# Expert stage of a transformer block: the second layer too by seven products of tiles in place of eight

## The reference, cut to what matters

```
h = jax.nn.relu(jnp.einsum('ecd,edf->ecf', buf, w1) + b1[:, None, :])          # d = 256, f = 1024
y = (jnp.einsum('ecf,efd->ecd', h, w2) + b2[:, None, :]) * (1.0 - MOE_TOKEN_DROPOUT)   # dropout 0.2
return g1[:, None] * y1 + g2[:, None] * y2
```

## Time and profile before

| | us |
| --- | --- |
| runs | 5859.25, 5866.38, 5866.96; median 5866.38 |
| the profiled execution | 5857.93, its span 5856.2 |
| busy, of the span | PE 5507.3 (94%), PEld 4313.5 (74%), DVE 4335.1 (74%), ACT 3283.8 (56%), POOL 2037.6 (35%) |
| second layer's matmuls (L1489) | 926.0, 15% of the chain that ended last |
| one gather on POOL (L1663), mean | 1.05 |
| mean granted TensorE clock | 0.985 |

### The profile page before, as it was taken

The page is one execution under the profiler, slowest core; times in us unless marked ns, Lnnn a source line. Parts: engine busy times, 40 slices in busy tenths (PEclk is TensorE's granted clock), DMA queues, the critical chain, the costliest instruction groups (busy, mean ns, idle before and its releaser), DMA issues. The chain is left out here.

```text
span 5856.2 us, 150644 instructions
## 1 busy us (share of the span) xinstructions
PE 5507.3 (94%) x45977; PEld 4313.5 (74%) x45977; DVE 4335.1 (74%) x11737; ACT 3283.8 (56%) x7315; POOL 2037.6 (35%) x1753
## 2 busy tenths in 40 slices
PE   0999999979999999799999999977899999999998
PEld 0677777757777777567777777753788888888887
DVE  7889898868888888588888888879555555455554
ACT  4788888746666666477777777747223232232322
POOL 0222222223333333234444444430334343333433
PEclk9999999989999999899999999998999999999999
DMA  5777777646666666466676767642322222222221
GB/s 154 180 181 182 183 184 182 169 135 175 173 173 175 174 173 175 115 166 181 168 181 169 179 170 180 170 113 2 71 54 41 52 50 39 51 48 41 55 38 24
DMA packets 625563, 750.63 MB, mean 128 GB/s; under 512 B 131075, under 2 KB 554188, under 8 KB 625328
## 3 DMA queue, kind: packets, MB, share of 16 engines
q1 hardware_dynamic: 568992, 679.62, 44.3%
q0 software_dynamic: 49152, 63.10, 6.7%
q10 hardware_dynamic: 7184, 5.00, 0.4%
HBM read 476.49 MB, written 272.24 MB: 128 GB/s over the span
## 5 line engine op out<-in xcount | busy, mean ns | idle before, releaser
L1489 PE MATMUL exp_res<-exp_w,exp_hT 128*128 128x256 f32 x4096 | 926.0, 380 | 0.0
L1489 PEld LDWEIGHTS exp_res<-exp_w,exp_hT 128*128 128x128 f32 x4096 | 769.8, 190 | 97.9
L1682 POOL DMA_INDIRECT out_dram<-exp_gated,exp_token x256 | 406.2, 1587 | 990.8 <-issue 357.0
L931 DVE TENSOR_REDUCE F_tops<-F_score 128x2 f32<-128x512 f32 x1024 | 684.4, 687 | 60.8 <-PE F_score L685 41.1
L822 ACT ACTIVATE F_probs<-F_scoreT 128x512 f32<-128x512 f32 x1024 | 583.7, 590 | 235.8 <-PE F_scoreT L654 235.8
L931 DVE TENSOR_REDUCE A_tops<-A_score 128x3 f32<-128x384 f32 x1024 | 531.6, 554 | 63.7 <-PE A_score L671 55.5
L1545 ACT ACTIVATE exp_lone<-exp_lead 128x256 f32<-128x256 f32 x256 | 98.3, 384 | 766.5 <-PE exp_lead L1499 747.9
L822 ACT ACTIVATE A_probs<-A_scoreT 128x384 f32<-128x384 f32 x1024 | 451.2, 488 | 23.5 <-PE A_scoreT L642 14.9
L1539 ACT ACTIVATE exp_hT<-exp_hT,exp_b 128x512 f32<-128x512 f32 x512 | 339.3, 712 | 92.6 <-DVE exp_hT L1625 92.6
L654 PE MATMUL F_scoreT<-QS,KS 98*128 98x256 bf16 x2048 | 365.3, 275 | 9.6 <-ACT F_probs L822 1.5
L685 PE MATMUL F_score<-KS,QS 96*128 96x256 bf16 x2048 | 363.4, 275 | 8.7 <-DMA KS<-d_k 7.8
(11 more groups left out here) (357 smaller groups left out, 14519.1 us busy)
## 6 DMA issues: line engine op xcount, KB each, us to landing
QS<-d_q SPq DMA_DIRECT2D x384, 192.0 KB, 3.6
KS<-d_k SPq DMA_DIRECT2D x256, 192.0 KB, 4.0
QS<-d_q SPq DMA_DIRECT2D x384, 128.0 KB, 3.9
KS<-d_k SPq DMA_DIRECT2D x256, 128.0 KB, 4.0
d_q<-A_q_parts SPq DMA_DIRECT2D x64, 384.0 KB, 3.5
d_k<-A_k_parts SPq DMA_DIRECT2D x64, 384.0 KB, 3.8
QS<-d_q SPq DMA_DIRECT2D x384, 64.0 KB, 3.6
d_q<-X_q_parts SPq DMA_DIRECT2D x64, 384.0 KB, 3.9
```

Source lines behind the costliest of these rows:

```text
L931: nc.vector.tensor_reduce(dst, src, AX.X, ALU.max).then_inc(score_read, 1)
L1489: last = mm(res[t][:, s, :], hT[par][:, f, (2 * t + s) * P:(2 * t + s + 1) * P], w2[k][:, f, :], start=begin and f == fs[0], stop=f == BY_ ...
L1682: nc.gpsimd.indirect_dma_start(out, bass.IndirectOffsetOnAxis(token[j % (2 * XB)][:, s:s + 1], 0), gated[par][:, s, :], None, bounds_check ...
```

## The change

The second layer gets the same scheme as the first. Rows are taken in halves of 256 (two row tiles q), the 1024 inner columns in halves of four tiles (u, u + 4), the 256 output columns in halves of 128. A product of halves is 4 x 2 matmuls with 128 moving columns (`add`), and there are seven of them. `fold_second` makes the four sums `w2s` of quarters of `w2` once an expert (in chunk 5 for the next one; `fold_weights` moves from chunk 6 to chunk 4). `raise_sums` makes four sums `hTs` of quarters of `hT` each chunk: for tiles 0 to 2 in operations of 768 columns, then for tile 3 in operations of 256. The PSUM tiles `lead[0]` and `corner` are used again for the second layer, beside new `side_r` and `last_r` in place of `res`. ACT copies `lead[0]` out twice (`lone_r`, `pair_r`), takes over the two copies of `turn` from DVE (`copy_half`) and the four multiplications by the gate (`weigh`), which it does in the next chunk. DVE joins the four quarters of `y` with six sums, and scales `y` in place (`scale_rows`), the second half of it in the next chunk. ACT's last turn of the loop is peeled. Constants used before the expert stage move to an inner allocation (`program`), which makes room for the new tiles.

```diff
-        res = [ps(f"res{i}", [P, 2, 256]) for i in range(2)]
+        side_r, last_r = ps("side_r", [P, 2, HR]), ps("last_r", [P, 2, HR])
...
# PE
+                        def rows_of(f, half):
+                            return lambda q: hT[par][:, f, half * HR + q * P:half * HR + (q + 1) * P]
+                        def sums_of(s, u):
+                            return lambda q: hTs[:, s, u, q * P:(q + 1) * P]
+                        def tile(f, d):
+                            return w2[k][:, f, d * P:(d + 1) * P]
+                        def add(region, weights, moving, begin=False, end=False):
+                            for q in range(2):
+                                last = mm(region[:, q * P:(q + 1) * P], weights(q), moving, start=begin and q == 0, stop=end,
+                                          skip_group_check=True)
                             return last
+                        def straight(u):
+                            pe.wait_ge(hid_read, NF * n + 2 * u + 1)
+                            add(lead[0], rows_of(u, 0), tile(u, 0), u == 0)
+                            pe.wait_ge(hid_read, NF * n + 2 * u + 2)
+                            return add(corner, rows_of(u + HF, 0), tile(u + HF, 0), u == 0, u == HF - 1)
+                        def outer(u, ready, begin=False):
+                            pe.wait_ge(raised, 8 * n + ready)
+                            add(side_r[:, 0, :], sums_of(0, u), w2s[k][:, 0, u, :], begin, u == HF - 1)
+                            pe.wait_ge(raised, 8 * n + ready + 1)
+                            add(side_r[:, 1, :], sums_of(2, u), w2s[k][:, 2, u, :], False, u == HF - 1)
...
-                        need(pe, res_read, 2 * n)
-                        products(0, 0, BY_PAIR[0:4], True)
+                        need(pe, pair_kept, HF * n + HF - 1)
+                        need(pe, corner_read, HF * n + HF)
+                        for u in range(HF - 1):
+                            straight(u)
                         close(HF - 1)
-                        products(0, 0, BY_PAIR[4:6], False)
                         if another(n):
                             rows_here(r, j + 1)
                             turn_half(j + 1, n + 1, 0)
-                        products(0, 1, BY_PAIR[0:6], False)
-                        products(0, 0, BY_PAIR[6:8], False)
-                        products(0, 1, BY_PAIR[6:8], False).then_inc(res_full, 1)
+                        if c == 0:
+                            pe.wait_ge(folded2, 4 * e + 4)
+                        need(pe, res_read, 2 * n)
+                        for u in range(HF - 1):
+                            outer(u, 1, u == 0)
+                        straight(HF - 1).then_inc(res_led, 1)
+                        outer(HF - 1, 5)
                         if another(n):
                             turn_half(j + 1, n + 1, 1)
-                        products(1, 0, BY_PAIR, True)
-                        products(1, 1, BY_PAIR, True).then_inc(res_full, 1)
+                        pe.wait_ge(res_kept, n + 1)
+                        pe.wait_ge(raised, 8 * n + 7)
+                        for u in range(HF):
+                            last = add(lead[0], sums_of(1, u), w2s[k][:, 1, u, :], False, u == HF - 1)
+                        last.then_inc(res_full, 1)
+                        pe.wait_ge(raised, 8 * n + 8)
+                        for u in range(HF):
+                            add(last_r[:, 0, :], sums_of(3, u), tile(u + HF, 1), u == 0, u == HF - 1)
+                        for u in range(HF):
+                            last = add(last_r[:, 1, :], rows_of(u + HF, 1), w2s[k][:, 3, u, :], False, u == HF - 1)
+                        last.then_inc(res_closed, 1)
# ACT
+                            if u == 1 and earlier:
+                                weigh(n - 1, 1 - par, 0)
                             if u > 1:
                                 rectify(u - 2)
+                            if u == 2 and earlier:
+                                weigh(n - 1, 1 - par, 1)
...
                         rectify(HF - 2)
+                        if another(n):
+                            copy_half(n + 1, 1 - par, 0)
                         rectify(HF - 1)
+                        act.wait_ge(res_led, n + 1)
+                        need(act, res_corner, n)
+                        nc.scalar.activation(lone_r[:, :], lead[0][:, :], ACT.Copy).then_inc(res_kept, 1)
+                        if another(n):
+                            copy_half(n + 1, 1 - par, 1)
+                        act.wait_ge(res_full, n + 1)
+                        need(act, res_read, 2 * n)
+                        nc.scalar.activation(pair_r[:, :], lead[0][:, :], ACT.Copy).then_inc(res_pair, 1)
# DVE
+                def raise_sums(n, par, us, done, which):
+                    a11, a12 = hT[par][:, us, 0:HR], hT[par][:, us.start + HF:us.stop + HF, 0:HR]
+                    a21, a22 = hT[par][:, us, HR:NS], hT[par][:, us.start + HF:us.stop + HF, HR:NS]
+                    m = [hTs[:, i, us, :] for i in range(4)]
+                    if which == 0:
+                        v.tensor_tensor(m[0], a21, a22, ALU.add).then_inc(raised, 1)
+                        v.tensor_tensor(m[2], a11, a21, ALU.subtract).then_inc(raised, 1)
+                    else:
+                        dve.wait_ge(raised, 8 * n + done + 1)
+                        v.tensor_tensor(m[1], m[0], a11, ALU.subtract).then_inc(raised, 1)
+                        dve.wait_ge(raised, 8 * n + done + 3)
+                        v.tensor_tensor(m[3], a12, m[1], ALU.subtract).then_inc(raised, 1)
...
+                            if u == 0 and not (isinstance(n, int) and n == 0):
+                                scale_rows(n - 1, k if c else 1 - k, 1 - par, 1)
+                            if u == 0 and isinstance(n, int) and n == 0:
+                                fold_second(0, 0)
                             if u < HF - 1:
                                 first_corner(n, par, u + 1)
+                            else:
+                                dve.wait_ge(hid_read, NF * n + NF - 2)
+                                raise_sums(n, par, slice(0, HF - 1), 0, 0)
                             dve.wait_ge(closed, HF * n + u + 1)
...
-                        if another(n):
-                            copy_half(n + 1, 1 - par, 0)
+                        raise_sums(n, par, slice(0, HF - 1), 0, 1)
+                        dve.wait_ge(hid_read, NF * n + NF)
+                        raise_sums(n, par, slice(HF - 1, HF), 4, 0)
+                        raise_sums(n, par, slice(HF - 1, HF), 4, 1)
+                        dve.wait_ge(res_kept, n + 1)
+                        need(dve, gated_ready, 2 * n - 2)
+                        v.tensor_tensor(corners[0], by_tile(corner[:, :]), by_tile(lone_r[:, :]), ALU.add).then_inc(res_corner, 1)
...
-                        dve.wait_ge(chosen, 3 * n + 3)
+                        dve.wait_ge(res_pair, n + 1)
+                        v.tensor_tensor(third_r[:, :], side_r[:, 1, :], pair_r[:, :], ALU.add).then_inc(res_joined, 1)
+                        v.tensor_tensor(both_r[:, :], side_r[:, 0, :], pair_r[:, :], ALU.add).then_inc(res_joined, 1)
+                        dve.wait_ge(res_joined, 2 * n + 1)
+                        v.tensor_tensor(corners[3], by_tile(side_r[:, 0, :]), by_tile(third_r[:, :]), ALU.add).then_inc(res_read, 1)
+                        dve.wait_ge(res_closed, n + 1)
+                        dve.wait_ge(res_joined, 2 * n + 2)
+                        v.tensor_tensor(corners[1], by_tile(last_r[:, 0, :]), by_tile(both_r[:, :]), ALU.add)
+                        v.tensor_tensor(corners[2], by_tile(last_r[:, 1, :]), by_tile(third_r[:, :]), ALU.add).then_inc(res_read, 1)
+                        if another(n):
+                            first_corner(n + 1, 1 - par, 0)
                         dve.wait_ge(biases, 2 * e + 2)
-                        for t in range(2):
...
+                        scale_rows(n, k, par, 0)
+                        if not another(n):
+                            scale_rows(n, k, par, 1)
```

More of the change, by code:

```diff
@@ L1393, in experts @@
         xTs = [sb(f"xTs{i}", [P, 4, HR]) for i in range(2)]
+        w2s = [sb(f"w2s{i}", [P, 4, HF, P]) for i in range(2)]
+        hTs = sb("hTs", [P, 4, HF, HR])
+        lone_r, pair_r, both_r, third_r = (sb(n, [P, HR]) for n in ("lone_r", "pair_r", "both_r", "third_r"))
         lone, pair, both = [[sb(f"{n}{i}", [P, HR]) for i in range(2)] for n in ("lone", "pair", "both")]
@@ L1540, in rectify, with weigh, copy_half @@
                                     .then_inc(hid_read, 1)
+                        def weigh(n, par, t):
+                            act.wait_ge(scaled, 2 * n + t + 1)
+                            if t == 0:
+                                act.wait_ge(chosen, 3 * n + 3)
+                                need(act, added, 64 * (n - 1))
```

(42 more changed lines are left out.)

92 lines of the change are left out of this document (39 added, 53 removed).

## The result

The changed kernel takes 5791.23 us (median of 4 runs, 5789.98 to 5792.88), the kernel before 5865.18 (4 runs); the ratio is 0.9876, 95% interval 0.9859 to 0.9893. That is 74 us less. Forecast were 5787 in a range of 5762 to 5832, and 80 us less.

What follows compares the result with a forecast made beforehand. PE, by how fast it can start records, was taken to bound the expert stage. Over 64 chunks -89 us, plus 7.8 at the end and 1.5 at the start, gave -80: 5787 us, range 5762 to 5832.

Steps and rivals of the forecast that it cites:

- Price of a record: Second layer on PE: each 128-column record costs 0.111 us, the pace of weight loads; gain 1.39 us a chunk.
- rival by columns: Second layer: columns alone set the pace, 0.108 us a record, 1.72 us a chunk gained, 5766 us; chance 11%.
- uncovered loads: Second layer: weight loads don't overlap matmuls, period 34.3 us, +480 us, 6355 us in all; chance 2%.
- Period: One regular chunk of the expert stage: 25.39 us in place of 26.80.
- Handovers: Between engines inside a chunk: PE never waits, though each slack is only 0.2 to 0.8 us.
- slack at the seam: VectorE's work past the chunk's end: slack 0.6 us, less the token copy of 0.17.
- Rival 2: At the seam between chunks VectorE becomes the bound; 2.0 us later, the gain is gone; chance 7%.
- The ends: Costs paid once: 1.5 us in the first chunk, 7.8 us after PE's last matmul.
- The stall stays: Where the expert loop turns back: the wait of some 6 us stays, with no cost added.
- rival 1: Handovers late in the chunk: a wait of 0.5 us a chunk costs 32 us, 5819 us; chance 25%.

Runs made afterwards that it cites:

- e1: Changed kernel with 64 moving columns in place of 128 in 44 of the second layer's 56 matmuls a chunk, same weight loads; 5789.3 us.
- e2: Changed kernel with second-layer operands swapped: 28 matmuls of 256 columns in place of 56 of 128, half the weight loads, same columns; 5763.6 us.
- e5: Changed kernel with one more unread 768-column VectorE sum a chunk, at the seam between chunks ahead of scale_rows; 5802.8 us.
- e6: Changed kernel with two more unread 768-column VectorE sums a chunk, at the seam between chunks ahead of scale_rows; 5856.3 us.
- e7: Changed kernel with the expert stage's loop over pairs of experts written out, so no engine turns back; 5784.1 us.
- e4: Kernel before with only ScalarE's part of the change (copies of turned rows, gates), second layer still with eight products; 5863.4 us.

## Why the prediction was right

It was right in direction, size and mechanism. Point by point:

- **Price of a record.** The sum stood on 0.111, read off a matmul of 8 columns elsewhere in the kernel; measured are 0.1115 to 0.1117. e1 and e2 change columns and loads one at a time and show that the loads set it. The rival by columns (0.108, 5766) is refuted by both, that of uncovered loads (6355) by the records themselves: loads that fill all rows and show as 0.19 us stand 0.1115 apart with the matmuls in flight beside them. The Trainium skill ("TensorE: Matmul & The Clock Gate", section "The mechanism") says that a load overlaps a matmul in flight only when the row groups differ; this trace doesn't agree. The Trainium skill's columns / 1.2 for a load, 107 ns for 128 (same page, section "LDWEIGHTS (loading the stationary operand)"), is near but below the 111.5 ns seen; by it the estimate was 118 us for the chunks, where 84 were measured.
- **Period.** 25.39 forecast, 25.48 measured. The 0.09 us is the largest miss: 0.0006 us on 112 records, and the rounding of 0.216 and 0.108. Over 64 chunks it is 5 of the 8 us by which the stage's gain of 72 stays behind the 80 forecast; the loop's turn is 3 more. That the medians are only 4 us from the forecast 5787 is in part luck: the forecast started from a median of 5866.4 and the comparison has 5865.2, and the stages ahead of the experts vary by several us.
- **Handovers.** None was late in a regular chunk. The steps of the schedule came within 0.3 us, the later ones early: `exp_both` waits as before for `pair`, S3 of tiles 0 to 2 ends at 5022.29, 17.7 after the chunk's start as forecast. A 768-column sum takes 0.95, starts 0.88 to the next; two `gated` on ACT take 0.90 together, 0.40 from the first's start to the second's, where 0.45 was taken. ACT is busy 45% of the stage, where about 50% was forecast. The slack at the seam was put at 0.6 less 0.17, so 0.43; e5 measures it as 0.88 - 0.19 = 0.7 (the period is 0.19 longer), 0.3 more than forecast.
- **Rival 2, VectorE at the seam.** Its price was right: 2.0 us more at the seam were to undo the gain, and 1.76 more left a ratio of 0.9991. By e5 and e6 the slack of 0.7 and the gain of 1.32 a chunk add up to 2.0 as well; the forecast had 0.6 and 1.39.
- **The ends.** First chunk 1.5 forecast, 1.7 measured, of which 1.3 have the cause that was named; the other 0.4 come from the lower clock level, which was at nothing in the sum. End 7.8 forecast, 8.0 measured.
- **The turn of the loop.** "The stall stays" was the one step that failed: it grew from 6.2 to 9.0 us. The 2.8 us more have three parts: PE itself now waits 1.8 us there for no semaphore, which it did for 0.6 before; its wait for VectorE is 4.5 us in place of 3.6; and the lower clock level after it costs 2.3 in place of 1.5. That a long wait costs more than itself was said under rival 1, with the row, but it stands in no term of the sum. Written out (e7) the whole 9 us go. Why the two waits grew is not shown; PE's loop holds more instructions now.

## What to carry to other kernels

Before a scheme that trades columns for more, narrower matmuls, look up in the trace what the narrowest matmul with a full weight load costs: that is the floor. Here it is 0.1115 us, and at 0.216 us for 256 columns about 132 columns cost as much (an estimate from the two), so 128 columns lie just below it. Judge an engine that takes over hidden work by the slack of each handover in the chunk, not by its busy share; 78% busy cost 1.1 us a chunk and 82% cost 0.2; the 0.7 us of slack at one seam decided. And where a change moves work past the last matmul, price the end apart: edits to it, to the first chunk and to the turn of the loop took out 18 us here that the steady chunk doesn't show. A wait also costs what the lower clock takes after it: 2.3 us behind one of 4.5.

## What was not expected of the hardware

Sixteen matmuls of 64 columns took 1.73 us, 0.108 each, and some groups of four 0.39 us, where four usually take 0.45. The loads are not faster beside a short matmul: in e1 the loads of the second layer start 0.111 to 0.112 us apart, and so do the matmuls, but for one gap of 0.058 us in each of the five stretches of narrow matmuls of a chunk. Twice a chunk the width goes back to 128 columns behind such a stretch, and there one gap of 0.165 stands: 0.058 + 0.165 are two gaps of 0.1115.

The turn of the loop cost 8.0 to 12.0 us in seven traces of kernels with the changed kernel's loop, and 6.2 and 6.1 in the kernel before and in e4, so it varies by more than some of the effects measured here.
